# VectorE's order around the W2 product: first evictions ahead of two quarter sums, the fourth sum later, the second product's wait split by bank; the second pair's narrow split moved

## The reference, cut to what matters

```
x = x + einsum('bct,bcd->bdt', x, w0[adapter])                       # layer 0
x = x + x @ W1 + (x @ A1[adapter].T) @ B1[adapter]                   # layer 1
x = x + x @ W2.T + 0.5 * (x @ A2[labeler].T) @ B2.T                  # layer 2
x = x + x @ W3.T + 2 * sum over two experts of gate * (x @ A3.T) @ B3   # layer 3
```

## Time and profile before

| | before |
|---|---|
| median of 3 runs | 528.64 us (528.32 to 529.77) |
| the profiled execution | 530.39 us |
| its span | 528.5 us |
| mean granted TensorE clock | 0.993 of full speed |
| PE busy | 519.0 us, 98% of the span |
| DVE, ACT, POOL busy | 334.5, 201.3, 169.9 us |

### The profile page before, as it was taken

One profiled execution on the slowest core, in us unless ns is written; L12 is line 12 of the kernel. 1 busy time (PEld: TensorE's weight loads), 2 busy tenths in 40 slices (PEclk: granted clock), 3 DMA queues, 4 the chain that ended last, 5 costly groups with the idle time before them and its releaser, 6 DMA issues.

```text
span 528.5 us, 8849 instructions
## 1 busy us (share of the span) xinstructions
PE 519.0 (98%) x2716; PEld 452.2 (86%) x2716; DVE 334.5 (63%) x654; ACT 201.3 (38%) x349; POOL 169.9 (32%) x250
## 2 busy tenths in 40 slices
PE   8997999999999999999999999999999999999997
PEld 8997999998888888888888788888888888888885
DVE  4795797599823333279876964756747647466464
ACT  5642553346232323267444333233233333233322
POOL 2540100002111111128746525453354444542400
PEclk9997999999999999999999999999999999999999
DMA  8910410203440202040602313313232142132312
GB/s 274 374 42 1 96 40 1 79 1 107 148 171 2 81 0 81 0 160 7 209 31 76 106 55 114 121 41 111 83 106 89 58 129 84 59 95 80 119 31 79
DMA packets 29343, 46.80 MB, mean 89 GB/s; under 512 B 12020, under 2 KB 17396, under 8 KB 29188
## 3 DMA queue, kind: packets, MB, share of 16 engines
q1 hardware_dynamic: 29124, 45.85, 26.4%
q0 software_dynamic: 192, 0.59, 0.3%
HBM read 33.39 MB, written 13.04 MB: 88 GB/s over the span
## 4 chain that ended last, share of the span: by engine, by line
PE 84%; DVE 5%; SPq 3%; DMA 3%; issue 2%; POOL 1%; POOLq 1%; ACT 1%; DVEq 0%
PE bank L1865 26%; PE bank L1799 13%; PE bank L1731 11%; PE bank L1854 7%; PE bank L1773 5%; PE bank L1785 5%; PE bank L1913 4%; PE bank L1921 4%; PE bank L1686 2%; DMA w2raw<-in_w_dram 2%; DVE em_lo L1165 2%; PE bank L1916 1%; PE bank L1915 1%; DVE w2raw L1222 1%; PE bank L1928 1%
## 5 line engine op out<-in xcount | busy, mean ns | idle before, releaser
L1865 PE MATMUL bank<-t_hi,em_hi 128*128 128x512 f32 x168 | 57.4, 403 | 0.0
L1165 DVE TENSOR_TENSOR w1t_lo<-raw,w1t_hi 128x1024 fp32r<-128x1024 f32 x18 | 24.4, 1355 | 23.4 <-ACT w1t_hi L897 17.1
L672 POOL TENSOR_TENSOR tmp<-raw 128x512 f32<-128x512 f32 x4 | 7.2, 1790 | 97.6 <-DVE raw L1349 97.6
L1865 PEld LDWEIGHTS bank<-t_hi,em_hi 128*128 128x128 f32 x168 | 31.2, 189 | 7.2 <-DVE em_hi L1165 0.4
L1799 PE MATMUL bank<-te,em_hi 128*128 128x512 f32 x144 | 34.9, 395 | 0.0
L658 POOL CAST em_hi<-tba 128x256 fp32r x32 | 13.9, 464 | 62.6 <-PE bank L1854 59.0
L1799 PEld LDWEIGHTS bank<-te,em_hi 128*128 128x128 f32 x144 | 27.0, 188 | 6.6
L1165 DVE TENSOR_TENSOR em_hi<-tmp,em_hi 128x512 fp32r<-128x512 f32 x22 | 15.1, 687 | 21.7 <-ACT em_hi L1004 12.6
L662 POOL TENSOR_TENSOR em_lo<-tba,em_hi 128x256 fp32r<-128x256 f32 x32 | 28.1, 897 | 2.4 <-POOL em_hi L658 1.2
L1731 PE MATMUL bank<-em_hi,w2s_hi 128*128 128x384 f32 x80 | 27.0, 337 | 0.0
L1731 PE MATMUL bank<-em_lo,w2s_hi 128*128 128x384 f32 x80 | 27.0, 337 | 0.0
(11 more groups left out here) (293 smaller groups left out, 1617.2 us busy)
## 6 DMA issues: line engine op xcount, KB each, us to landing
raw<-in_x_dram SPq DMA_DIRECT2D x16, 512.0 KB, 4.0
b1s<-b1scr SPq DMA_DIRECT2D x32, 217.5 KB, 2.7
raw<-in_b1w_dram SPq DMA_DIRECT2D x10, 512.0 KB, 3.3
out_dram<-ef SPq DMA_DIRECT2D x16, 256.0 KB, 2.0
out_dram<-ost SPq DMA_DIRECT2D x16, 256.0 KB, 2.4
graw<-in_w3a3wr_dram SPq DMA_DIRECT2D x4, 768.0 KB, 10.9
b1scr<-b1stage SPq DMA_DIRECT2D x12, 256.0 KB
w2raw<-in_w_dram SPq DMA_DIRECT2D x7, 384.0 KB, 6.1
```

The source lines that it names most:

```text
L1165: V.tensor_tensor(dst, src, f32(hi), ALU.subtract).then_inc(signal, 1)
L1865: ins = nc.tensor.matmul(to[:, :], left[a][:, k0 + k, :], m_right(right, z, k), start=(name in OPENS and n == 0), stop=(n == 3 * KH - 1), ...
```

## The change

In the W2 stage VectorE does `early_lo(0)` to `early_lo(5)` before the sum s2, `early_lo(6)` after s2, and `early_lo(7)` after t1; the sum s4 goes behind t3. TensorE waits for all three b2 evictions before p5 no longer at once: bank 4 + j waits for `s_accl` of 8 + j (K is 8). In pair 1 `xn_lo(b1)` goes in front of `sum_p1`; the other pairs keep their order.

```diff
             quad_lo("b21", 0, KQ)
+            for n in range(OUTER):
+                early_lo(n)
             w2_sum("s2", "s1", "a11", ALU.subtract, "s3")
-            w2_sum("s4", "a12", "s2", ALU.subtract, "s2")
+            early_lo(OUTER)
             dve.wait_ge(s_g3[Q_LOAD["b12"]], 16)
             dve.wait_ge(s_diag, Q_DIAG["b12"])
             dve.wait_ge(s_g3l, Q_SPLIT["b11", 0])
             t_sum("t1", "b12", "b11", None)
-            for n in range(K):
-                early_lo(n)
+            early_lo(OUTER + 1)
...
             t_sum("t3", "b22", "b12", "t1")
+            w2_sum("s4", "a12", "s2", ALU.subtract, "s2")
             w2_sum_lo("s2")
...
                     split_lo("t4", BACK)
+                    xn_lo(b1, YB)
                 sum_p1(p)
                 operand_lo(CS[1], raw[1][:, 0:KH, :], CS[0], ops + 5)
                 sum_p5(p)
-                xn_lo(b1, YB)
+                if not after_first:
+                    xn_lo(b1, YB)
...
-            pe.wait_ge(s_accl, ACC_P)
             pe.wait_ge(s_wsl, W_SPLIT["s1"])
             pe.wait_ge(s_tsl, T_SUM["t1"])
             for j in range(KQ):
+                pe.wait_ge(s_accl, K + j)
                 g_product("p5", YBANK, j, True)
```

## The result

The changed kernel takes 523.64 us (median of 4 runs, 523.05 to 525.11); the kernel before, run beside it on the same chip, 529.2 us (4 runs, 528.32 to 531.56). The ratio is 0.9892, with a 95% interval of 0.9853 to 0.9931, which leaves out 1: faster by 5.6 us. The forecast was 522.65, the range 521.4 to 524.4. The profiled execution took 525.11 us, its span is 523.1 us (before: 528.5).

What follows compares the result with a forecast made beforehand. TensorE, busy 98%, was taken as the bound, leaving its waits and clock to gain from. From the 528.64 us median, less 3.43 (wait) and 2.85 (slow clock), plus 0.3 (pair 1), came 522.65 us, range 521.4 to 524.4.

Steps and rivals of the forecast that it cites:

- The wait of 3.43 us: TensorE's idle time ahead of the first b2 product in the W2 stage, to go whole: 3.43 us gained.
- Rival E: The W2 wait hangs on b2's split, or VectorE's PSUM reads slow TensorE: no change, 528.6 us, chance 0.03.
- The slow stretch, 2.85 us: Matmuls at half clock behind the W2 wait, to return to full clock: 2.85 us gained.
- Rival C: The slow stretch is smaller in unprofiled runs or part of it stays: 524.1 us with half, chance 0.17.
- The sum: Whole kernel: all terms together take 5.98 us off the 528.64 us median, giving 522.65 us.
- Why it fell: W2 stage: the clock fell to half after 2.5 us of TensorE standing still, costing 2.85 us.
- Rival D: The clock falls anyway, or through a new gap such as pair 1's 1.0 us stand: 525.5 us, chance 0.09.
- Half-quarter splits at 0.2 of cover: Splits of b12 and b22 for the third b2 product, about 0.2 us early: cost nothing, at most 0.2.
- Bank-wise waits worth nothing: Separate waits by bank at p5: worth nothing by themselves, some tenths when a staging transfer lands late.
- Rival F: t1's low split slips and TensorE stands at p5: slower, 530 us at a stand of 4.5 us, chance 0.04.
- s4 later, worth nothing: s4 behind t3 on VectorE: its low split about 1.4 us late, cover over 6 us, cost nothing.
- Pair 1, +0.3: The 0.89 us won at `mixed` is given back and VectorE slips 0.2 to 0.5 us: 0.3 us lost.

Runs made afterwards that it cites:

- e4: The kernel before with t1 put behind the first six evictions, s2 and s4 still in front: 525.69 us, ratio 0.9931.
- e7: The kernel before with s4 alone put behind all eight evictions, s2 and t1 in front: 525.53 us in one run.
- e2: The kernel before with only pair 1's edit, `xn_lo(b1)` ahead of `sum_p1`: 529.21 us, ratio 0.9993.
- e8: The kernel before with 32 unused 128-column transposes in TensorE's stand ahead of the b2 product: 530.17 us, ratio 1.0012.
- e10: The kernel before with ten unused 128-column transposes in TensorE's stand ahead of the b2 product: 527.78 us, ratio 0.9971.
- e5: The changed kernel with s4 back directly behind s2, six evictions still in front: 524.84 us, ratio 0.9915.
- e3: The changed kernel with the old single wait for all three b2 evictions put back before p5: 523.54 us, ratio 0.9886.
- e1: The changed kernel with pair 1 in its old order, so the W2 part alone: 524.19 us, ratio 0.9891.
- e6: The changed kernel with the splits of t2 and t4 earlier in pair 1 and `xn_lo(b1)` back in its old place: 524.18 us, ratio 0.9897.
- e11: e9 with t4's splits behind the first block's gates and `xn_lo(b1)` behind the sums again in pair 1: 523.34 us, ratio 0.9886.
- e9: The changed kernel with ScalarE's copy of B3 moved behind h2T in the first pair: 523.81 us, ratio 0.9899.

## Why the prediction was right

*The wait of 3.43 us.* Right: it went whole, and e4 and e7 show that it shrinks with the sums that stand ahead of the evictions (3.3, 1.8, 1.0, 0). Rival E is out with it, for the wait followed the evictions, and these didn't slow TensorE.

*The slow stretch, 2.85 us.* The mechanism was right and the size was one execution's, not the kernel's. The profiled execution of before had 2.9 us of it, that of e2 1.5; an average run pays 2.0 by the clocks of 47 runs, and 2.2 (1.3 to 3.0) by e4. Rival C had this: "the slow stretch is smaller in unprofiled runs". The two runs of before that kept the full clock took 527.5 us, 3.9 over the changed kernel's 523.64, close to the 3.43 of the wait alone.

*The sum.* That the forecast came within 1.0 us is in part luck. The slow stretch was put 0.85 us too high and pair 1's cost 0.3 us too high, and the two errors have opposite signs: 5.98 - 0.85 + 0.3 = 5.4, where 5.56 was measured. The rest of the distance between 522.65 and 523.64, 0.56 us, is the other base: the runs beside the change had 529.2 for the kernel before, not 528.64.

*Why it fell.* "The fall in the rows follows 2.5 us of standing still" was a reading of one execution. e8 shows that the fall goes away when TensorE works in the stand, e4 that a single stand of 1.8 us left the clock alone in four runs, and e10 that two shorter stands with a little work between them brought it down in four runs of twelve, by the mean clocks. The stand of 3.3 us did so in 45 of 47. Rival D was wrong for the case at hand: TensorE's new stand of 0.56 us in pair 1 left the clock at 1.00, and so did the 0.99 us of e7. The Trainium skill, "TensorE: Matmul & The Clock Gate", section "A second HAM failure mode: psum-queue depth-cycling", on which D leaned, warns of repeated short idles. No run here shows that: each kept trace has at most one fall before its last three microseconds, and the changed kernel, whose stands are few, has none.

*Half-quarter splits at 0.2 of cover.* Right, 0.2; e5's profile shows what a cover that is gone cost there, 0.3 us.

*Bank-wise waits worth nothing.* Right within 0.1 us (e3). The last b2 eviction ended at 58.06, not 56.95. Of these 1.1 us, 0.8 is p1's later start in this execution (49.59 for 48.77); the other 0.3 is a real slip, which took the cover of 0.2 away: ScalarE, which stands for a store of the staging buffer ahead of the second and the third of these evictions, stood 3.06 us for the first of these stores, 2.69 before. Rival F feared such a slip, and needs TensorE to stand 3.4 us for it.

*s4 later, worth nothing.* Right about its deadline (its low split ended at 72.86, ten microseconds ahead of p3 at 83.2). Not seen was that, left in front, it costs time at the half-quarter splits, 0.3 us in e5's profile.

*Pair 1, +0.3.* The mechanism was right (0.43 of idle time, `mixed` on time, the stand passed to `gated_across`), the size wrong: 0.0, because the gates' small steps took 0.52 us less. The text put this at most at 0.3 ("a later start meets less of it"). The stand at `gated_across` was 0.56 us, not 1.0, for the same reason. What it left out is that GpSimd's work moves too. In the five profiles with the new order, GpSimd's low splits there begin 1.0 us ahead of the gates' first step, and the gates take 1.87 to 1.89 us up to gh; in five with the old order they begin 0.06 to 0.07 us behind it, and the gates take 2.37 to 2.39. Half of that shift is the gates' later start, and the other half GpSimd's: its casts just ahead of these splits take 1.37 us, with the old order 1.92 to 1.94. e1 lies between (0.3 us ahead, 2.02 us), and in e6 and e11 they begin 0.8 us behind it, with 2.33 us for the gates. No run moves GpSimd alone, so this is a pattern over the profiles and not a test. On such slowness beside GpSimd, e6 is the clear case, with 2.81 against 1.29 us and 1.78 against 0.68. The Trainium skill, "SBUF — State Buffer", section "Who interferes with whom", says that a VectorE instruction with two inputs in SBUF contends with GpSimd's reads; the splits of t4 and GpSimd's sum are such a pair, and these rows agree; they also fit the prediction's sentence that one engine blocks the other whole.

*What was missed*: the start, which differed by 0.87 us between the two profiles, and the late load of B3. Both differ between executions of one kernel, and e9 shows for the second that the median hardly feels it.

## What to carry to other kernels

When an engine's queue holds both something that TensorE waits for and something due much later, put the first in front, and then check what is next: here the wait went whole because every cover up to p1 was at least 0.2 us, and e5's profile shows that one step left in the wrong place takes 0.3 back. A split moved ahead of a sum only moves a wait if the chain behind it is as late (pair 1: 0.9 us won, 0.9 given back); taking other work out of that chain made pair 1 0.6 us shorter in e11's profile. And a penalty read from one profile, such as a slow clock, is one execution's: compare the mean granted clock of several runs before putting it into a sum, or before saying what an experiment such as e10 showed.

## What the runs showed of the hardware

- The clock stayed at 2.4 GHz over single stands of 0.6, 1.0 and 1.8 us, and fell to 1.2 GHz in stands of 3.3 and 3.5 us, 2.5 to 3.3 us after TensorE's last matmul. It also fell with two stands of 1.55 and 1.15 us and ten 128-column transposes between them. By the mean clocks it isn't the same in every run: the kernel with the stand of 3.3 us kept the full clock in 2 of 47 runs, the one with ten transposes in 8 of 12, and the one with 32 transposes in 10 of 10.
- The half clock then lasted from about 43.0 to 49.9 us in one execution, and from 44.8 to 48.2 us in another of the same code in that stage (e2). The runs of the kernel before fall into the same two groups, 20 and 25 of 47, 1.1 us apart in their medians.
- A GpSimd sum of 128x512 floats took 1.29 us beside small steps of VectorE and the beginning of a split, and 2.81 us beside its splits of t4; a VectorE split of 128x512 took 0.68 us and 1.78 us.
- ScalarE, which runs in order, stood up to 4.2 us for a store of an output buffer, and passed 1.7 us of it on to TensorE through a copy that had nothing to do with the buffer.
